# Two-layer graph network on one core: the last product by Strassen's scheme, layer-1 input finished a step earlier, low parts of hT on GpSimd

## The reference

```python
h  = relu(layernorm(x))
w  = adj * exp(q(h) @ k(h).T);  w = w / w.sum(2)
x1 = x + w @ (h @ Wv.T + bv)                      # layer 0
h1 = relu(layernorm(x1))
A  = adj + I;  d = A.sum(-1) ** -0.5
y  = x1 + (d_i * A * d_j) @ (h1 @ W + b)           # layer 1, out
```

## Time and profile before

| | |
|---|---|
| median of three runs | 1636.63 us |
| profiled execution, its time | 1638.41 us |
| profiled execution, its span | 1636.6 us |
| PE busy | 1623.8 us (99%) |
| DVE busy | 1345.8 us (82%) |
| ACT busy | 1075.1 us (66%) |
| POOL busy | 800.9 us (49%) |
| mean granted TensorE clock | 0.997 |

### The profile page before, as it was taken

One profiled execution on the slowest core, in us unless ns is written; L12 is line 12 of the kernel. 1 busy time (PEld: TensorE's weight loads), 2 busy tenths in 40 slices (PEclk: granted clock), 3 DMA queues, 4 the chain that ended last, 5 costly groups with the idle time before them and its releaser, 6 DMA issues.

```text
span 1636.6 us, 37843 instructions
## 1 busy us (share of the span) xinstructions
PE 1623.8 (99%) x12061; PEld 1546.9 (95%) x12061; DVE 1345.8 (82%) x3370; ACT 1075.1 (66%) x2450; POOL 800.9 (49%) x970
## 2 busy tenths in 40 slices
PE   9899999999999999999999999999999999999999
PEld 7799999999999999999999999999999999999998
DVE  6888888888888888888888888888888888888886
ACT  5666766766766766666667667667667666666663
POOL 3454554455455445445545544554554454454452
PEclk9999999999999999999999999999999999999999
DMA  6365465464454554554554554654544545545531
GB/s 184 94 149 139 112 150 128 112 158 125 118 154 124 123 152 120 129 151 113 137 144 110 146 130 111 159 125 115 155 124 121 152 122 127 151 116 134 148 87 49
DMA packets 494559, 212.66 MB, mean 130 GB/s; under 512 B 402512, under 2 KB 427344, under 8 KB 494544
## 3 DMA queue, kind: packets, MB, share of 16 engines
q1 hardware_dynamic: 492624, 210.89, 50.8%
q10 hardware_dynamic: 1920, 1.58, 0.3%
HBM read 146.28 MB, written 66.13 MB: 130 GB/s over the span
## 4 chain that ended last, share of the span: by engine, by line
PE 95%; DVE 2%; SPq 1%; ACT 1%; issue 0%; POOL 0%; DMA 0%; POOLq 0%; DVEq 0%; ACTq 0%
PE ps L971 32%; PE ps L973 32%; PE ps L974 32%; SPq L180 1%; DMA adj_blocks<-in_adj_dram 0%; DVE g_lo L665 0%; ACT unused_x L467 0%; DVE ht_lo L769 0%; DVE unused_a L930 0%; DVE w_lo L659 0%; DVE z_lo L752 0%; DVE p_lo L810 0%; DVE v L691 0%; SPq L210 0%; DVE late L785 0%
## 5 line engine op out<-in xcount | busy, mean ns | idle before, releaser
L444 ACT ACTIVATE g_hi<-ps,u_col 128x256 fp32r<-128x256 f32 x256 | 105.6, 464 | 311.7 <-PE ps L974 311.7
L304 POOL TENSOR_TENSOR xb<-xb,bv_row 128x512 f32<-128x512 f32 x128 | 163.3, 1298 | 283.2 <-DVE late L758 267.3
L971 PE MATMUL ps<-ht_hi,m_hi 128*128 128x256 f32 x1024 | 286.8, 280 | 0.0
L973 PE MATMUL ps<-ht_lo,m_hi 128*128 128x256 f32 x1024 | 286.6, 280 | 0.0
L974 PE MATMUL ps<-ht_hi,m_lo 128*128 128x256 f32 x1024 | 286.4, 280 | 0.0
L971 PE MATMUL ps<-w_hi,z_hi 128*128 128x512 f32 (+1 forms) x516 | 203.1, 394 | 0.7 <-DVE z_lo L752 0.7
L974 PE MATMUL ps<-w_hi,z_lo 128*128 128x512 f32 (+1 forms) x516 | 202.8, 393 | 0.0
L973 PE MATMUL ps<-w_lo,z_hi 128*128 128x512 f32 (+1 forms) x516 | 202.5, 393 | 0.0
L971 PEld LDWEIGHTS ps<-ht_hi,m_hi 128*128 128x128 f32 x1024 | 193.3, 189 | 0.0
L974 PEld LDWEIGHTS ps<-ht_hi,m_lo 128*128 128x128 f32 x1024 | 193.2, 189 | 0.0
L973 PEld LDWEIGHTS ps<-ht_lo,m_hi 128*128 128x128 f32 x1024 | 193.1, 189 | 0.0
(11 more groups left out here) (165 smaller groups left out, 5507.8 us busy)
## 6 DMA issues: line engine op xcount, KB each, us to landing
x_in<-in_x_dram SPq DMA_DIRECT2D x64, 512.0 KB, 5.0
xb<-in_x_dram SPq DMA_DIRECT2D x64, 512.0 KB, 4.5
out_dram<-late SPq DMA_DIRECT2D x127, 256.0 KB, 2.1
h_scratch<-h SPq DMA_DIRECT2D x62, 512.0 KB, 2.8
...
adj_blocks<-in_adj_dram SPq DMA_DIRECT2D x256, 64.0 KB, 2.5
...
```

The source lines that it names most:

```text
L304: last = pool.tensor_tensor(xb[:, t, :], xb[:, t, :], bv_row[:], ALU.add)
L444: last = act.activation(g_hi[:, m, :], ps[:, G + j, m % 2 * N:m % 2 * N + N], ACT.Identity, bias=u_col[:, m:m + 1])
L971: pe.matmul(dst, a_hi[:, c, cols], b_hi[:, c, :], start=(first and c == 0), stop=False, skip_group_check=not first)
L973: pe.matmul(dst, a_hi[:, c, cols], b_lo[:, c, :], start=False, stop=False, skip_group_check=not first)
```

## The change

Five things are changed.

1. The product with W goes by the same scheme of seven products that V uses. W's quarters and four sums of them are prepared once, in step 1, on POOL (`w_sums`, four sums, and `w_high`) and in step 2 on DVE (`w_low`). Per graph there are four sums of quarters of Z (`z_sum`, made on DVE), their high parts (ACT, `z_sums_high`) and their low parts (DVE for S1 and S2, POOL for S3 and S4). The seven products R1 to R7 take 42 matmuls of 256 columns. R1, R2, R4 and R5 stand between S and PV, R6 between PV's two halves, R7 and R3 behind PV. DVE adds their results into y in eight pieces of 128x256 (`part`).
2. `keep_x1` runs at the end of the step in which PV is made, no longer at the head of the next. Its sum of x1 is taken by the same instruction, and the squares are summed on ACT (`x1_squares`). `bn_stats` and `bn_aggr` are gone from the steady steps.
3. `ht_lo` is made on POOL at the end of its step.
4. POOL's order at the head of a step: `row_norms` and the power `rs` come ahead of `hat_low`. At the end of the step POOL waits for `v_lo_ready[2]` before its low part of Z's sums.
5. DVE's order: `sums_of_l` stands between the two halves of `z_low`; `value_low_upper` and `value_low_lower` stand behind `p_low`.

The core of the diff:

```diff
             def step(this, prev, main, ahead, older=True, second=True):      # GpSimd
                 if prev and older:
-                    diagonal_ones(this - 1, main)
+                    diagonal_ones(this - 1)
                     if main:
                         ht_sums_low(this)
+                        pool.wait_ge(d_ready, this - 1)
+                        pool.wait_ge(dn_turned_ready, this - 1)
+                        row_norms(this)
+                        pool.wait_ge(ve_1_done, this - 1)
+                        pool.tensor_tensor(rs_1[:], ve_1[:], minus_half[:], ALU.pow).then_inc(rs_1_done, 1)
                     hat_low(this - 1, older)
...
+                if main and prev and older:
+                    z_sums_low_second(this - 1, this)
+                if main and ahead and prev:
+                    for j in range(2):
+                        pool.wait_ge(ht_hi_ready[j], this + 1)
+                        pool.tensor_tensor(ht_lo[:, 2 * j:2 * j + 2, :], ht[:, 2 * j:2 * j + 2, :],
+                                           ht_hi[:, 2 * j:2 * j + 2, :].bitcast(fp32),
+                                           ALU.subtract).then_inc(ht_lo_by_pool[j], 1)
...
+            def z_sums_low_second(graph, this=None):
+                if this is not None:
+                    pool.wait_ge(v_lo_ready[2], this)
+                pool.wait_ge(z_sum_hi_ready, 2 * graph)
+                pool.tensor_tensor(z_sum_lo[:, S3:S4 + 1], z_sum[:, S3:S4 + 1], z_sum_hi[:, S3:S4 + 1].bitcast(fp32),
+                                   ALU.subtract).then_inc(z_sum_lo_by_pool, 1)
...
+            def w_sums():                                                     # GpSimd, once
+                pool.tensor_tensor(w_parts[:, T1], w_parts[:, T3], w_parts[:, B11], ALU.subtract).then_inc(w_sum_ready, 1)
...
+            def w_high():
+                pool.tensor_copy(w_hi[:, 0:4], w_parts[:, 0:4])
+                pool.tensor_copy(w_hi[:, 4:7], w_parts[:, 4:7]).then_inc(w_hi_ready, 1)
+                for block in (T2, T3):
+                    pool.tensor_tensor(w_lo[:, block], w_parts[:, block], w_hi[:, block].bitcast(fp32), ...
...
+            def z_low_second(graph):                                          # VectorE
+                dve.wait_ge(z_hi_ready[1], graph)
+                dve.tensor_tensor(z2_lo[:].rearrange("p c n -> p (c n)"), ps[:, Z + 1, :],
+                                  z2_hi[:].rearrange("p c n -> p (c n)").bitcast(fp32),
+                                  ALU.subtract).then_inc(z_lo_ready[1], 1)
+                dve.tensor_tensor(z_sum[:, S1], z_rows[1][:, :, P:N], z21[:], ALU.add).then_inc(z_sum_ready, 1)
+                dve.wait_ge(z_sum_ready, 4 * graph - 2)
+                dve.tensor_tensor(z_sum[:, S2], z_sum[:, S1], z_rows[0][:, :, 0:P], ALU.subtract).then_inc(z_sum_ready, 1)
+                dve.wait_ge(z_sum_ready, 4 * graph - 1)
+                dve.tensor_tensor(z_sum[:, S4], z_rows[1][:, :, 0:P], z_sum[:, S2], ALU.subtract).then_inc(z_sum_ready, 1)
...
-                if main and ahead and prev:
-                    ht_low(this + 1, None)
...
+                if main and ahead:
+                    dve.wait_ge(xb_ready, this)
+                    keep_x1(0, this)
+                    if prev:
+                        upper_right_begin(this - 1, d)                        # R6
+                    keep_x1(1, this)
+                    if prev:
+                        x1_mean(this)
+                        lower_end(this - 1, d)                                # R7, twice
+                        upper_right_end(this - 1, d)                          # R3, y_ready[0]
...
+            def first_parts(graph, older=True, this=None):                    # TensorE
+                part(R1, YA, (z1_hi, z1_lo), whole, B11)
+                pe.wait_ge(e_ready[0], this)
+                part(R2, YE, (z2_hi, z2_lo), upper, B21)
+                pe.wait_ge(e_ready[1], this)
+                part(R4, YD, (z2_hi, z2_lo), lower, T4)
+                pe.wait_ge(z_sum_lo_ready, graph)
+                part(R5, YC, z_sums(S1), whole, T1)
```

More of the change, by code:

```diff
@@ L501, in step @@
                     hat_high(this - 1)
+                if main and prev and older:
+                    x1_squares(this)
                 if main and not prev:
@@ L552, in step @@
                 if prev and older:
-                    z_high(this - 1)
+                    z_high_first(this - 1)
+                    if main and second:
+                        x_square_half(0, this + 2)
+                    z_high_second(this - 1)
+                if prev and not main:
+                    z_sums_high(0, this - 1)
+                    z_sums_high(1, this - 1)
                 if main:
@@ L558, in step @@
                     if second and prev:
[L559 removed]
+                        if not older:
+                            x_square_half(0, this + 2)
+                        x_square_half(1, this + 2).then_inc(x_square_ready, 1)
                     for t in range(NT):
@@ L906, in step @@
                 if prev and older:
-                    z_low(this - 1)
+                    z_low_first(this - 1)
+                    if main:
+                        sums_of_l(this, prev)
+                    z_low_second(this - 1)
+                if prev and not main:
+                    z_sums_low_first(this - 1)
                 if main:
-                    value_low_upper(this)
-                    value_low_lower(this)
                     if second and prev:
                         x_variance(this + 2)
+                    if not prev or not older:
+                        value_low_upper(this)
+                        value_low_lower(this)
                     dve.wait_ge(adjt_ready, this)
@@ L1065, in values, with part @@
                 value(V3, VC, sums(S4), whole, B22, HD, first=False)
[L1067 to L1081 removed]
+            def part(k, bank, left, cols, block, first=True):
+                product(ps[:, bank, 0:HD], 2, left, cols, (w_hi[:, block], w_lo[:, block]), first).then_inc(r_done[k], 1)
@@ new lines, in third_part, with sixth_part @@
+            def third_part(graph, older=True):
+                pe.wait_ge(z_sum_lo_by_pool, graph)
+                pe.wait_ge(y22_begun, graph)
+                weights_ready(older, 5)
+                part(R3, YC, z_sums(S4), slice(0, P), B22, first=False)
+            def sixth_part(graph, older=True):
+                pe.wait_ge(y11_begun, graph)
+                if not older:
+                    pe.wait_ge(w_lo_by_pool, 2)
+                part(R6, YA, z_sums(S2), slice(0, P), T2, first=False)
@@ L1083, in last_graph, with seventh_part @@
+            def seventh_part(graph):
+                pe.wait_ge(z_sum_lo_by_pool, graph)
+                pe.wait_ge(y12_begun, graph)
+                part(R7, YA, z_sums(S3), slice(0, P), T3, first=False)
             def last_graph(graph):
                 pe.wait_ge(y_ready[0], graph - 1)
+                pe.wait_ge(y_ready[1], graph - 1)
                 for k in range(14):
-                    pe.matmul(ps[:, O1, 0:N], p_hi[:, 0, 0:P], p_hi[:, 1, :], start=True, stop=True)
+                    pe.matmul(ps[:, YA, 0:N], p_hi[:, 0, 0:P], p_hi[:, 1, :], start=True, stop=True)
@@ L1174, in step @@
                         pe.wait_ge(consts_ready, 2)
-                    for part in v_lo_ready:
-                        pe.wait_ge(part, this)
+                    for lower_part in v_lo_ready:
+                        pe.wait_ge(lower_part, this)
                     pe.wait_ge(v12_ready, this)
```

411 lines of the change are left out of this document (262 added, 149 removed).

## The result

The changed kernel takes 1872.46 us (median of four runs, 1863.74 to 1873.73) against 1636.79 for the kernel before: 1.1425 times as long, with an interval of 1.141 to 1.144. The direction and the closed chain were forecast; the size was not (1723, range to 1750). The profiled execution has a span of 1871.1 us.

What follows compares the result with a forecast made beforehand. Prediction: PE bounds the kernel before; after the change a closed POOL and DVE chain does. 62 x (26.1 - 24.83) = +78.7, start +7, end +1, together +86.7, give a median of 1723 us, range 1645 to 1750.

Steps and rivals of the forecast that it cites:

- the closed chain: POOL from V to hat_lo's end, then DVE back to V, repeating every step: 10.24 + 15.74 = 25.98 us.
- PE's own work: W product by 42 short matmuls takes 0.56 us less; a step of 24.27 us if PE never waits.
- The chain and its signs: POOL and DVE set the step; signs: PE waits before PV and R4, DVE idles before the transpose, steps 26 us apart.
- POOL's part: POOL's queue from V (value_low_lower done) to the end of hat_lo, without waiting for PE: 10.24 us.
- the forecast idle time: DVE idle in front of the adjacency transpose until POOL's hat_lo is done: 0.5 to 1 us.
- DVE's part: DVE from hat_lo's end to V, summed from the earlier kernel's rows: 15.69 us and 0.05 to react.
- A rule speaks for more: POOL and DVE contend for SBUF, stretching DVE by 0.1 to 0.3 us a step; left out of the sum.
- 2.87 us of cover: PE's R1, R2, R4, R5 between S and PV, hiding the p, p_hi, p_lo trip; 5.58 us stood there before.
- Late x_in: Load of x_in behind y's later second store delays ACT's sums: 0 to 0.4 us a step, 0.12 taken.
- Start: Extra POOL work in step 1 and later low parts of hT for step 3: +7 us, bounds 0 and 14.
- Clock: Rival: waits each step drop PE to the 1.2 GHz level for a stretch, 1847 us; chance 0.03.
- the end: The last graph's W product has the trip Z, sums, high, low inside it: +1 us.

Runs made afterwards that it cites:

- e2: d4 with DVE's two sums over l and its four sums of Z cut to two columns each; 1693.36 us.
- c1: b2 with DVE's sums over l moved behind the second half of z_low, and z2's high part ahead of x's squares on ACT; 1726.18 us.
- b1: Separate small kernel timing DVE's instruction forms alone and beside POOL; tensor_tensor with both inputs in SBUF took 0.62 us alone, 1.47 beside POOL.
- a4: Changed kernel with SP issuing the two stores of y behind the loads of xb and x_in; 1818.06 us.
- b2: a4 with POOL's hat_lo waiting until DVE's nb is done, and g_low(0) ahead of the transpose of the adjacency; 1755.87 us.
- d4: c1 with POOL's ht_lo and ht_sum_lo cut to two columns, constants for x1's mean, squares and y's scale, and d copied ahead of x1; 1724.57 us.
- c2: c1 with ht_lo back on DVE behind V's low parts, and POOL waiting for it before z_sum_lo; 1751.06 us.
- d2: c1 with POOL's ht_lo and ht_sum_lo cut to two columns each; 1724.10 us.
- b3: Changed kernel with the product with W done directly by 24 matmuls of 512 columns, as before the change; 1731.69 us.
- a2: Changed kernel with DVE's sums_of_l moved from between Z's low parts to behind V's low parts; 1874.32 us.
- a1: Changed kernel without POOL's wait for v_lo_ready[2] before the low part of Z's sums; 2149.43 us.
- d1: b3 with the load order of a4, the edits of b2 and the place of the sums over l from c1; 1647.65 us.

## Why the prediction was wrong

- **PE's own work: not contradicted.** No run had PE free of waits in the seven-product form, so 24.27 was never seen as a step. e2 less its wait is 25.51 - 1.01 = 24.50, which holds short gaps too.
- **The chain and its signs: right in kind, not in every sign.** POOL's part is 10.51 for 10.24. `z_sum_lo` starts at V. PE waits before R4 for e and before PV for `v_lo`, 1.22 where 1.5 to 2 were named. PE busy fell to 90%, not 93 to 95: the wait before R2 was not forecast (`z_lo` is late behind the sums over l). Two things that were to prove the prediction wrong are there: POOL idles 0.31 for d inside the stretch, and DVE's transpose waits for nothing (808.96), since `sc` ends with `hat_lo`. Where `sc` stands alone, in c1, the forecast idle time shows: DVE stands 0.77 until `hat_lo` is done at 851.68.

```profile
850.38 1.30 POOL L368 TENSOR_TENSOR hat_lo<-adjt,hat_hi 128x512 fp32r<-128x512 f32 x1 [0.55 <-DVE nb L1036]
```

```profile
851.77 0.71 DVE L842 STREAM_TRANSPOSE adjt<-adj_blocks 128x512 f32<-128x512 f32 x1 [0.77 <-issue]
```

- **DVE's part: the step that failed.** The prediction put it at 15.74, "by starts of successive rows" of a kernel in which POOL stood elsewhere. It measured 17.73, and with POOL's 0.27 more this is the whole step of 28.25 where 25.98 were summed. Of the 1.99 more, 1.94 can be read off: the second sum +0.48 and `v22` +0.19, beside `ht_sum`; the wait for `dn_row` 0.54; and 0.73 by `sc`, which ends no sooner than `hat_lo`: the transpose starts 0.20 later, and ACT's h1 comes so late that `h_lo` starts 0.13 and `v_u` 0.40 later. `sc` and `nb` weren't in the sum, since they seemed to lie beside `hat_lo` for nothing.
- **"A rule speaks for more": read the right way, priced wrongly.** The contention that the Trainium skill states (GPSIMD Engine Reference, section Specifications), which b1 agrees with in kind (0.62 to 1.47), was put at 0.1 to 0.3 a step from one pair of rows, 0.93 against 0.74, and left out of the sum. It and what goes with it cost 28.38 - 25.93 = 2.45 us a step: 0.90 by the order of the loads (a4), 1.01 by b2, 0.54 by c1. None of the three edits takes away meetings alone: a4 also ends the waits for x_in and `dn_row`, b2 moves `g_low(0)`, c1 moves a copy on ACT. The bound from a row that is only grazed isn't the bound for a tiny instruction that meets a whole one, 1.23 us (b1).
- **One chain too few.** The forecast had seen 2.87 us of cover, but booked the wait as part of POOL's chain. The trip from S to PV is a limit of its own at 25.5 (e2), and DVE's stretch from Z to V one at 25.95 (d4), both within 0.6 us of the forecast's 26.1; the way through PV, x1 and d binds only in c2, at 26.35, and its length without c2's edit wasn't measured. So where the step did come down to the forecast's size, POOL's chain wasn't what held it: c1 is 25.93, and with two of that chain's passes cut (d2) it is 25.95. That c1's number is near 26.1 is luck.
- **Late x_in: too small.** 0.12 was taken, with 0.4 as the bound. ACT waited 2.6 us for x_in, and the order of the loads gave 0.90 a step (a4), the same 0.90 as above.
- **Start: mis-sized, within its bound.** +7 was forecast, bound 14. The first `hat_lo` (step 1) starts at 50.90 for 45.87, the second (step 3) at 95.47 for 83.60: +5.0, the preparation of W, then +6.8, 11.9 in all. In b3 the second is at 85.87, +2.3, so most of it comes with the seven products.
- **Clock: a small term.** Of the 59 steps between the third `hat_lo` and the 62nd, 42 ran wholly at a granted clock of 1.00, the 2.4 GHz level, with 28.21 us in the mean; 17 had a stretch at the lower level, 28.76: some 9 us in all. a2 and a4 ran at 0.99 and over, with the loss still there. With waits of 0.84 to 1.22 us the clock thus mostly stayed up; in a1, with 4.46 before PV, it is 0.91.

The sum in the prediction's own terms, by the starts of `hat_lo`: the 62 steps from the second to the last grew by 216.3 us (1533.1 to 1749.4) where 78.7 were forecast, the start by 11.9 for 7, the end by 6.3 for 1. Together this is the 234.5 us by which the span grew. No version that was run beats the kernel before. The best with seven products and nothing left out is c1, 1726; with the direct product in the same order it is d1, 1648 against 1637. So the seven products cost 79 us (c1 against d1) even with most meetings gone, 62 x (25.93 - 24.86) = 66 of it in the steps.
